# The last two groups' expert sums turned by VectorE and stored in blocks, instead of turned by TensorE

## What is computed

```
h  = layernorm(x) @ fc_in_w.T + fc_in_b
8 times:  h = h + dt * (alph * 0.5 * (adj @ h - h) + h @ w_eff - h + x0)
x1 = x + h
z  = layernorm(x1)
ffn = z;  for e in 0..7:  ffn = ffn + combine[:, e] * (gelu(z @ w1[e] + b1[e]) @ w2[e] + b2[e])
out = x1 + ffn
```

## Time and profile before

| | |
|---|---|
| median of 3 runs | 532.05 us (531.63 to 532.14) |
| time of the profiled execution | 531.63 us |
| its span, first to last instruction | 529.5 us |
| PE busy | 514.8 us (97%) |
| DVE busy | 439.4 us (83%) |
| ACT busy | 297.8 us (56%) |
| POOL busy | 112.8 us (21%) |
| granted TensorE clock, mean | 0.999 of full speed |

### The profile page before, as it was taken

How to read it: one execution, slowest core, us unless ns; L and a number is a source line. 1 busy time by engine, 2 the same in 40 slices (tenths; PEclk the granted TensorE clock), 3 DMA queues, 4 the chain that set the end, 5 groups by cost and what they waited for, 6 DMA issues and landing times.

```text
span 529.5 us, 9181 instructions
## 1 busy us (share of the span) xinstructions
PE 514.8 (97%) x2799; PEld 451.0 (85%) x2799; DVE 439.4 (83%) x1012; ACT 297.8 (56%) x533; POOL 112.8 (21%) x174
## 2 busy tenths in 40 slices
PE   5999999999999999999999999999999999999996
PEld 4687997997799888998899878988799888997775
DVE  6798777789967997789967997789977996589896
ACT  6324433449625884459535883459535882149584
POOL 1204004213150412212240412222240412021010
PEclk9999999999999999999999999999999999999999
DMA  4040011099326972198327962298327951161071
GB/s 133 2 119 1 0 41 40 27 269 225 61 59 146 287 141 61 45 264 209 59 59 175 265 137 59 59 275 188 55 59 196 242 99 20 45 228 49 2 239 41
DMA packets 139359, 62.04 MB, mean 117 GB/s; under 512 B 102614, under 2 KB 133964, under 8 KB 137420
## 3 DMA queue, kind: packets, MB, share of 16 engines
q1 hardware_dynamic: 139340, 61.81, 46.5%
HBM read 47.90 MB, written 13.89 MB: 117 GB/s over the span
## 4 chain that ended last, share of the span: by engine, by line
PE 83%; DVE 7%; DMA 3%; ACT 2%; issue 2%; SPq 2%; POOL 1%; DVEq 0%; ACTq 0%; POOLq 0%
PE bank L1126 21%; PE bank L1128 21%; PE bank L1127 20%; PE bank L1303 11%; PE bank L1310 6%; DMA x0q<-x_rows 2%; PE bank L1252 1%; DVE scs L670 1%; DVE bn L674 1%; DMA x_rows<-x 1%; ACT work L604 1%; DVE work L982 1%; SPq L338 1%; DVE Q L1094 1%; PE bank L1154 1%
## 5 line engine op out<-in xcount | busy, mean ns | idle before, releaser
L670 DVE TENSOR_TENSOR scs<-work,scs 128x512 fp32r<-128x512 f32 x132 | 98.6, 748 | 1.7 <-ACT scs L481 0.5
L604 ACT ACTIVATE work<-bank,cols 128x512 f32<-128x512 f32 x128 | 86.7, 678 | 16.0 <-PE bank L1128 15.8
L481 ACT ACTIVATE scs<-work 128x512 fp32r<-128x512 f32 x132 | 83.1, 630 | 20.4 <-DVE work L982 19.0
L1303 PE MATMUL bank<-scs,w2s 128*128 128x512 f32 x256 | 80.7, 396 | 0.0
L1128 PE MATMUL bank<-M,GT 128*128 128x384 f32 x192 | 64.2, 335 | 0.0
L1126 PE MATMUL bank<-M,GT 128*128 128x384 f32 x192 | 64.2, 334 | 0.0
L1127 PE MATMUL bank<-M,GT 128*128 128x384 f32 x192 | 64.2, 334 | 0.0
L982 DVE TENSOR_TENSOR work<-work,GT 128x512 f32<-128x512 f32 x90 | 60.9, 683 | 1.7 <-ACT work L604 0.9
L422 POOL TENSOR_TENSOR mv<-bn 128x8 f32<-128x8 f32 x16 | 6.9, 429 | 239.5 <-DVE bn L674 239.5
L1303 PEld LDWEIGHTS bank<-scs,w2s 128*128 128x128 f32 x256 | 47.7, 188 | 10.7
L481 ACT ACTIVATE GT<-bank 128x512 fp32r<-128x512 f32 x36 | 21.1, 595 | 58.3 <-PE bank L1128 55.7
(11 more groups left out here) (196 smaller groups left out, 1220.5 us busy)
## 6 DMA issues: line engine op xcount, KB each, us to landing
GT<-comb_rows SPq DMA_DIRECT2D x8, 1536.0 KB, 7.0
Q<-comb_rows SPq DMA_DIRECT2D x16, 512.0 KB, 7.1
GT<-comb_rows SPq DMA_DIRECT2D x7, 1024.0 KB, 5.7
xn<-in_x_dram SPq DMA_DIRECT2D x16, 256.0 KB, 4.0
GT<-comb_rows SPq DMA_DIRECT2D x7, 512.0 KB, 4.2
res_rows<-scr SPq DMA_DIRECT2D x12, 256.0 KB, 2.6
x_rows<-x SPq DMA_DIRECT2D x12, 256.0 KB, 2.6
x0q<-x_rows SPq DMA_DIRECT2D x24, 128.0 KB, 3.9
```

Source lines behind the costliest of these rows:

```text
L481: return nc.scalar.activation(dst, src, ACT.Copy)
L604: nc.scalar.activation(hid[:, i % 2, :], bank[UP_BANK[i % 3]][:, :], ACT.Gelu, bias=cols[:, B1_COL + e:B1_COL + e + 1]).then_inc(gelu_done, 1)
L670: return v.tensor_tensor(dst, src, hi.bitcast(FP32), ALU.subtract)
L1303: pe.matmul(bank[SUM_BANK[b]][:, :], w2s[:, k, e, :], scs[:, i % RING, 0, :], start=(e == 0 and k == 0), stop=False)
```

## The change

For groups 6 and 7 the way by PE is removed: `copy_sum`, `transpose_out`, `add_out`, `store`, their semaphores, banks and waits are gone. Group 6 now takes the way of groups 0 to 5 in full. Group 7 takes it too, with two differences: its second batch is added by DVE (`last_out`), which waits for POOL's addition of the first one, and its `keep_res` and `blocks_of_res` stand on SP behind the stores of group 6. The core of the diff:

```diff
@@ SP
             def expert_weights(h, g=None, more=False):
-                if more:
+                if g is not None:
                     keep_res(h)
...
-                if more:
+                if g is not None:
                     blocks_of_res(h)
...
             expert_weights(GROUPS - 1)
-            for h in range(GROUPS - 2, GROUPS):
-                store(h)
-            sp.wait_ge(out_stored, 1 + 128 * BY_PE + 32 * (GROUPS - BY_PE))
+            store_blocks(GROUPS - 2)
+            keep_res(GROUPS - 1)
+            blocks_of_res(GROUPS - 1)
+            store_blocks(GROUPS - 1)
+            sp.wait_ge(out_stored, 1 + 128 * GROUPS)
@@ POOL
             def residual(h):
                 pool.wait_ge(z_ready, GB * h + GB)
...
+                pool.wait_ge(out_add, 1 + GB * h)
                 nc.gpsimd.tensor_tensor(res, x1, z, ALU.add).then_inc(res_ready, 1)
...
-                if not first and not final:
+                if not first:
                     for b in range(GB):
                         turned_out(g - 1, b)
...
             iteration(GROUPS - 1, final=True)
             residual(GROUPS - 1)
+            turned_out(GROUPS - 1, 0)
@@ ACT
-                    if i == ITEMS - 4 and not more:
-                        copy_sum(h, 0)
...
-                if not more:
-                    copy_sum(h, 1)
@@ DVE
-            def add_out(h, b):
...
+            def last_out(h):
+
+                dve.wait_ge(y_turned, GB * h + GB)
+                dve.wait_ge(resq_in, 64 * h + 64)
+                dve.wait_ge(out_add, 1 + GB * h + 1)
+                turned = outs[:, 1, :, :].rearrange("p t c -> p (t c)")
+                v.tensor_tensor(turned, turned, resq[:, 1, :], ALU.add).then_inc(out_add, 1)
...
                     scale_item(h, i, g is None and i < REP_PE)
-                    if i == 0 and g is None:
-                        add_out(h - 1, 1)
                     if i >= 1:
                         item_low(h, i - 1)
...
-                    if i == ITEMS - 5 and more:
+                    if i == ITEMS - 5:
                         turn_y(h, 0)
                     if i - 1 in Z_AT and g is not None and not more:
                         low_z(g, Z_AT.index(i - 1))
...
-                if more:
-                    turn_y(h, 1)
-                else:
-                    add_out(h, 0)
-                    if g is None:
-                        add_out(h, 1)
+                turn_y(h, 1)
+                if g is None:
+                    last_out(h)
@@ PE
-                        if s == 1 and g is None:
-                            transpose_out(h - 1, 1)
...
-                        if i == 0 and g is None:
-                            pe.wait_ge(out_add, 1 + GB * h)
+                        if e == 0 and g is None:
+                            pe.wait_ge(y_turned, GB * (h - 1) + b + 1)
...
-                    if s == ITEMS - 1 and not more:
-                        transpose_out(h, 0)
...
-                elif g is None:
-                    transpose_out(h, 1)
```

More of the change, by code:

```diff
@@ L202, in build @@
         res_kept, resq_in, y_turned = sem("res_kept"), sem("resq_in"), sem("y_turned")
-        yt_copied, ot_mm = sem("yt_copied"), sem("ot_mm")
         out_add = sem("out_add")
@@ L224, in build @@
         Z_SCALE, Z_AT = 5, [8, 10]
-        BY_PE = GROUPS - 2
         ROUTE_AT = [0, 1, 3, 4]
@@ L230, in build @@
         ZT_FIRST = [7, 6]
-        ZT_BANK, OT_BANK, LG_BANK = [7, 3], [2, 0], 7
+        ZT_BANK, LG_BANK = [7, 3], 7
         x_v = x.rearrange("(g b) (t p) c -> g b p t c", b=GB, p=P)
@@ L275, in next_x @@
                 load_x(g)
[L277 to L280, removed]
             def store_blocks(h):
@@ L450, in residual @@
                 pool.wait_ge(z_ready, GB * h + GB)
[L451 to L454, removed]
-                else:
-                    pool.wait_ge(out_add, 1 + GB * h)
+                pool.wait_ge(out_add, 1 + GB * h)
                 nc.gpsimd.tensor_tensor(res, x1, z, ALU.add).then_inc(res_ready, 1)
@@ L555, in _ @@
                 high_lt(2, [2 + k])
[L557 to L562, removed]
             def high_z(turn, b, banks=ZT_BANK):
@@ L1261, in transpose_z @@
                 last.then_inc(zt_mm, 1)
[L1263 to L1267, removed]
             def replicate(h, i):
```

## The result

| | before | after |
|---|---|---|
| median of the runs taken together (7 each) | 532.05 us | 533.93 us |
| ratio, with its 95% interval | | 1.0039 (1.0030 to 1.0049) |
| time of the profiled execution | 531.63 us | 534.04 us |
| its span | 529.5 us | 532.1 us |
| PE, DVE, ACT, POOL busy | 514.8, 439.4, 297.8, 112.8 us | 515.3, 441.3, 296.0, 116.5 us |

The change makes the kernel slower by 1.9 us, 0.4%; 534.3 was forecast. PE's busy time hardly moves, and TensorE's granted clock is 0.998 against 0.999: the time is in waits at the end. Executions also differ by some tenths in their first part. POOL's first addition of iteration 6, which no kernel here touches, starts at 429.73 before and at 429.95 after.

The account below looks back on a forecast made before the run. PE, busy 97% of the span, was taken as the bound, with a 4.8 us tail behind its last product. The terms gave span 531.7 against 529.5; 2.2 on the median 532.05 made 534.25, say 534.3; range 532.6 to 537.0.

Parts of the forecast that it names:

- Step 1: Iteration 7, item 11: new DVE transposition and POOL addition hold a DVE scaling; routing to `comb_out` 1.5 us later.
- Step 2: Start of group 7's experts: first low part held by POOL's residual until 505.8, ending 506.3; everything behind 0.7 us late.
- Step 3: Group 7's items: PE-bound, PE ends at 525.0; new transposition at item 11, about 518.2, costs nothing.
- Step 4: SP's queue: block stores issued until 514.3, residual out by 517.4, reads 6.3 us, `resq` in at 523.8, POOL done 525.3.
- Step 5: The end: eight stores of 0.5 us instead of one, from 525.3, last at 528.8, landing 2.5 later; span 531.7.
- slower by much more: Rival: group 7's residual reads meet queued stores and take 11.2 us instead of 6.3; 539.2, chance 0.1.
- The same: Rival: iteration 7's hold misses, weights only 0.6 us late, reads land early; 533.0, chance 0.2.
- Faster: Rival: PE's path decides, `resq` before about 521, first low part passes ahead of POOL's residual; 530.7, chance 0.07.

Follow-up runs that it names:

- e4: The full change with POOL's addition of the residual to group 6's first batch cut from 512 columns to 1: 533.01 us, 1.0030.
- e11: The kernel before, with POOL's residual of group 7 cut into eight instructions of 128 columns instead of one of 1024: 530.85 us, 0.9977.
- e12: The full change, with POOL's residual of group 7 cut into eight instructions: 533.69 us, 1.0029.
- e3: The full change with group 7's residual written to DRAM ahead of group 6's stores instead of behind them: 534.31 us, 1.0047.
- e6: The full change with group 7's residual neither written nor read back; its additions read what is left of group 6's: 533.65 us, 1.0034.
- e8: The full change with group 7 stored by eight DMAs of 32 partitions in 512-byte pieces, rows not in order: 533.35 us, 1.0022.
- e7: The full change with group 7 stored by two DMAs, one per batch, in 512-byte pieces, rows not in order: 532.01 us, 1.0005.
- e5: The full change with the four stores of group 7's second batch issued from ACT's queue instead of SP's: 533.64 us, 1.0034.
- e10: The kernel before with group 7 alone in blocks, both its additions on DVE, last eight stores split five on SP, three on ACT: 532.25 us, 1.0006.
- e2: The kernel before with group 7 alone in blocks; group 6 leaves by PE as before: 533.42 us, 1.0031.

## Why the prediction was right

The forecast was 534.3 and slower; the median is 533.93. The sum gave 2.2 us more for the span and put the same on the median; the spans differ by 2.6 and the medians by 1.9, as the profiled execution was 0.42 under its median before and 0.11 over it after. Step by step, on the clock of the tail where two profiles are compared:

- **Step 1, the hold in iteration 7.** Right. The scaling took 1.48 us beside POOL's 1.29, the low part behind it came 1.5 us late, and the weight stores behind the routing 1.35 (71.45 against 499.83 - 429.73 = 70.10), for 1.5 forecast. e4 shows the cause: with the addition cut, the hold is gone and 0.8 of the delay with it; 0.5 is left for the transposition itself. DVE's row ended 0.55 behind POOL's here too. The rule that the prediction cites from the Trainium skill's page SBUF — State Buffer stands there in the section SBUF: two separate sides, not in the one it names; the held rows of this trace agree with it.
- **Step 2, the start of group 7's experts.** Right. The first low part takes 2.59 us, until 506.46; that is 76.5 against 75.9 (505.59 - 429.73), 0.65 later for 0.7. That POOL's residual would be ahead of it decided this, and it was, by 0.33 us.
- **Step 3, group 7's items.** Right. PE's last product is followed by DVE at 525.28, 95.3 against 95.0 for ACT's copy, 0.3 later, as summed. The transposition at item 11 came at 518.41 and waited for nothing. The cover for it was thinner than said, though: DVE's last low part ended at 524.69, 0.07 before PE's last product started, at 524.76.
- **Step 4, SP and the queue.** Two terms of it were mis-sized, in opposite directions. The eight block stores held SP until 515.99 in place of 514.3, and the residual's writes landed to release the reads at 519.41 in place of 517.4; the reads then took 5.35 us until POOL's addition started, not 6.3 (with which the prediction's own sum is 523.7, not 523.8). In all `resq` was in 0.9 later than forecast (0.7 on the tail's clock), at 524.7.
- **Step 5, the tail.** The shape was right, eight issues in a row of 0.5 us, the first at 526.06 for 525.3. The landing of the last one was 2.0 us, not the 2.5 that I took as the upper value of four; this gave back 0.5 of the 0.9. The sum, 531.7, met a span of 532.1, of which 0.2 is the later start of the tail. That it came so close is in part luck: three terms of steps 4 and 5 were off by 0.5 to 2.0 us and nearly cancelled.

On the rivals: "slower by much more" needed the reads to meet a full queue; they were issued when the residual had landed, and landed themselves after 2.9 to 3.9 us. "The same" needed the hold to miss; it didn't. "Faster" priced the first low part's passing ahead of POOL's residual at up to 1.9 us; with the hold gone, PE's path is 0.8 shorter in e11 and 0.5 in e12. It also rested on a shorter trip; e3 and e6 show that it wouldn't have come even then, since an earlier addition on POOL holds DVE's last items. This is the one thing that I had not priced: step 4 treated an earlier `resq` as a pure gain. In the full change the addition began at 524.76, 0.07 after DVE's last low part had ended, by luck of the order.

The Trainium skill's sentence on short pieces (DMA: Bandwidth & Descriptors, Specifications) had been put beside the sum as a reason for a slower end. e8 against the full change bounds it here: at most 0.8 us of the tail for 4,096 pieces of 128 bytes in place of 1,024 of 512, about half of it in the length of the issues and 0.2 in the landing. Whether a read-modify-write stands behind it, no run shows.

## What to carry to other kernels

At the end of a kernel count the DMAs behind the last result before you count the engine work that they save: here each further store was 0.5 us of issue, and eight in place of two were 1.8 us at equal pieces (e8 against e7) and 2.6 with the shorter pieces, while DVE's last addition came only 0.1 us earlier on the tail's clock. A transfer and an addition that are hidden in the steady loop must be priced anew in the last iteration, where nothing follows to hide them. And when one engine's long instruction holds another by a shared resource, cut it into short ones: beside POOL's eight short additions no DVE row was held by more than 0.1 us (0.77 in place of 0.68).

## What the runs showed that I had not expected

- Cutting one POOL instruction of 1,024 columns into eight of 128 stretched it from 2.38 to 5.31 us, yet made the whole kernel 1.2 us faster (e11), twice the 0.54 us that the profile lists as PE's wait. By the starts of PE's rows the stall was 0.8 us, which is the whole gain of the profile's tail; the other 0.4 of the medians lies within their interval (0.7 to 1.8 us).
- An issue on ACT's queue was slower than on SP's for the same four stores (2.39 against 1.95 us), and these landed after 2.6 to 3.0 us, against 2.0 on SP alone (e5). Where both queues were in use at once, SP's also took up to 3.0 (e5) and 3.1 (e10), so the longer landing goes with the sharing. Whether ACT's slower issue comes from its queue or from the sharing isn't separated.
- Keeping the residual of group 7 directly behind the broadcasts held SP itself: in e2 its two DMAs took 5.36 us to issue, in place of 1.06 in the full change, where the block stores had taken that wait on themselves (10.85 us for eight, against 4.14 for the eight at the end).

```profile
505.35 5.36 SPq L295 DMA_DIRECT2D res_rows<-scr  x2
```
